# Score banks that hold two heads for half the columns, and value products that wait for half of the exponentials

## What is computed

```python
att = jnp.einsum('bhtd,bhsd->bhts', q, k) / jnp.sqrt(D)
att = att + _alibi_causal_mask(T, H, x.dtype)[None]
att = jax.nn.softmax(att, axis=-1)
y = jnp.einsum('bhts,bhsd->bhtd', att, v)
x = x + ga * (y.reshape(B, T, C) @ W_proj + b_proj)
```

## Time and profile before

| what | value |
|---|---|
| median of 3 runs | 578.42 us (578.05 to 579.37) |
| span of the profiled execution, from its first to its last instruction | 575.7 us |
| own time taken for that execution | the median, so 2.7 us lie around the span |
| first group's exponentials begin, last group's end | 52.4 and 448.7 us |
| mixture of experts on PE | from 449.4 us on |
| busy share of PE, DVE, ACT, POOL | 86%, 79%, 70%, 30% |

### The profile page before, as it was taken

How to read it: one execution, slowest core, us unless ns; L and a number is a source line. 1 busy time by engine, 2 the same in 40 slices (tenths; PEclk the granted TensorE clock), 3 DMA queues, 4 the chain that set the end, 5 groups by cost and what they waited for, 6 DMA issues and landing times.

```text
span 575.7 us, 15493 instructions
## 1 busy us (share of the span) xinstructions
PE 496.4 (86%) x5876; PEld 264.6 (46%) x5876; DVE 451.9 (79%) x775; ACT 400.9 (70%) x775; POOL 169.9 (30%) x293
## 2 busy tenths in 40 slices
PE   4756878889999999998999999989988999999970
PEld 2422323333243343333334325234433798999970
DVE  3689899989988998998998998995687555554451
ACT  4922366668888888888898887888788656555530
POOL 3310000010103102320034101047057860870864
PEclk9965599999999999999999999999899999999995
DMA  6592111000011450031310000010132222333332
GB/s 158 201 305 65 30 50 36 1 2 4 7 34 34 100 231 3 2 148 32 81 38 3 3 2 2 8 29 9 56 106 63 74 74 61 111 106 91 108 98 66
DMA packets 38263, 37.86 MB, mean 66 GB/s; under 512 B 7088, under 2 KB 33904, under 8 KB 37560
## 3 DMA queue, kind: packets, MB, share of 16 engines
q1 hardware_dynamic: 35808, 32.26, 19.5%
q0 software_dynamic: 2048, 4.20, 2.4%
q10 hardware_dynamic: 336, 0.42, 0.2%
HBM read 20.05 MB, written 16.61 MB: 64 GB/s over the span
## 4 chain that ended last, share of the span: by engine, by line
PE 59%; ACT 9%; DVE 5%; issue 3%; POOL 1%; DMA 1%; ACTq 0%; POOLq 0%; DVEq 0%
PE pv L745 18%; PE b L778 13%; PE b L852 8%; PE b L869 7%; ACT probs L1296 7%; PE b L717 6%; DVE part L1013 3%; PE b L692 3%; ACT raw L1266 1%; POOL raw L1478 1%; PE b L843 1%; PE b L647 1%; PE b L664 1%; ACT rows L1272 0%; DMA raw<-y_scratch,spots 0%
## 5 line engine op out<-in xcount | busy, mean ns | idle before, releaser
L1296 ACT ACTIVATE probs<-b 128x512 f32<-128x512 f32 (+1 forms) x576 | 298.6, 570 | 79.6 <-PE b L692 36.5
L1013 DVE TENSOR_REDUCE part<-b 128x2 f32<-128x1024 f32 (+2 forms) x320 | 327.7, 1061 | 26.8 <-PE b L717 11.8
L745 PE MATMUL pv<-probs,v_cur 128*32 128x256 f32 (+1 forms) x2432 | 176.7, 372 | 0.3 <-ACT probs L1296 0.2
L778 PE MATMUL b<-aug 55*128 55x512 bf16 (+3 forms) x640 | 114.2, 355 | 25.5 <-ACT probs L1296 21.3
L717 PE MATMUL b<-aug 52*128 52x512 bf16 (+3 forms) x640 | 117.1, 366 | 17.4 <-DVE part L1013 15.1
L778 PEld LDWEIGHTS b<-aug 55*128 55x128 bf16 x640 | 37.0, 93 | 137.6 <-ACT probs L1296 131.5
L745 PEld LDWEIGHTS pv<-probs,v_cur 128*32 128x32 f32 x2432 | 50.2, 109 | 68.3 <-issue 40.7
L852 PE MATMUL b<-hTt,inverse 128*128 128x128 f32 x424 | 56.3, 276 | 0.8 <-ACT hTt L1317 0.8
L869 PE MATMUL b<-w2T_sb,hst 128*128 x424 | 56.2, 276 | 0.8 <-ACT hst L1323 0.8
L869 PEld LDWEIGHTS b<-w2T_sb,hst 128*128 128x128 f32 x424 | 51.6, 192 | 1.2 <-issue 1.1
L852 PEld LDWEIGHTS b<-hTt,inverse 128*128 128x128 f32 x424 | 51.5, 192 | 1.0 <-issue 1.0
(11 more groups left out here) (151 smaller groups left out, 374.2 us busy)
## 6 DMA issues: line engine op xcount, KB each, us to landing
xt<-slot_scratch SPq DMA_DIRECT2D x53, 64.0 KB, 1.9
y_scratch<-aug SPq DMA_DIRECT2D x53, 64.0 KB, 1.5
slot_scratch<-slots SPq DMA_DIRECT2D x3, 1024.0 KB, 7.1
aug<-q_scratch SPq DMA_DIRECT2D x6, 384.0 KB
aug<-k_scratch SPq DMA_DIRECT2D x6, 384.0 KB
w2T_sb<-in_w2T SPq DMA_DIRECT2D x1, 2048.0 KB, 7.4
aug<-in_w1T SPq DMA_DIRECT2D x8, 256.0 KB, 2.6
q_scratch<-pieces SPq DMA_DIRECT2D x4, 384.0 KB, 2.6
```

The lines of the kernel that those rows point to most:

```text
L745: return mm(pv[32 * hh:32 * hh + 32, c0:c1], v_cur[:, kb, hh, :], probs[:, step_ % 2, hh, at_:at_ + c1 - c0], start=(kb == 0 and c0 == 0), ...
L778: done.append(mm(pair[half][:, at_:at_ + w], k_aug[g % 2][n, b, kb * P:kb * P + P], q_aug[g % 2][n, b, (j + 1) * CW - w:(j + 1) * CW], sta ...
L1013: ins = nc.vector.tensor_reduce(dst, b1[:, slot:slot + 2, at_:at_ + w], AX.X, ALU.max)
L1296: nc.scalar.activation(probs[:, p % 2, hh, 0:w], b2[:, (n2 - 1) % RING2, 0:w], ACT.Exp).then_inc(exp_done, 1)
```

## The change

A bank of scores held one head of a pair for all columns of the step. Now it holds both heads of one row tile (both low heads, or both high heads) for half of the columns, the same halves that `VALUE_PARTS` gives to the value products. `scores` is written as a generator for one row tile, and `alternate` interleaves the low and the high one, matmul by matmul. Each of the two banks waits for its own slot of the ring, just ahead of its own first matmul, and each counts itself ready after its own last matmul. The exponential reads a bank as two blocks and writes them to two heads of `probs`. Each half of the value products waits for the two exponentials that made its columns. The maxima are rewritten in the same manner (`maxima`), and their instructions come out in the order that they had. The core of the diff:

```diff
+                def alternate(low, high):
+                    for _ in zip_longest(low, high):
+                        pass
+                def mask_out(bank, half, at_, table, h, cols):
+                    k = slice(HALF * half, HALF * half + HALF)
+                    c0, c1 = cols
+                    return mm(bank[:, at_ + c0:at_ + c1], identh[k, h, :], table[k, h, c0:c1], start=False, stop=True, skip_group_check=True)
...
                 def value_products(p, b):
+                    pe.wait_ge(exp_done, HG * (NSTEP * g_ + q) + 2 * (b + 1))
                     if b == 0:
-                        pe.wait_ge(exp_done, HG * (NSTEP * g_ + q + 1))
...
-                def scores(p, b):
+                def scores(p, b, half):
                     j, kbs = STEPS[p]
-                    for half in range(2):
-                        wait_slot(half)
-                    pair = [b2[:, (len(freed) + half) % RING2, :] for half in range(2)]
+                    n = slice(HALF * half, HALF * half + ROWS2)
+                    wait_slot(0)
+                    bank = b2[:, len(freed) % RING2, :]
+                    n_exp[0] += 1
+                    freed.append((exp_done, n_exp[0]))
+                    parts = VALUE_PARTS[p][b]
                     at_ = 0
-                    for kb in kbs:
-                        w = width(j, kb)
...
-                    done[-1].then_inc(s2_ready, 2)
+                    for pair in range(PAIRS):
+                        for kb, _, c0, c1 in parts:
+                            w = c1 - c0
+                            ins = mm(bank[:, at_:at_ + w], k_aug[g % 2][n, pair, kb * P:kb * P + P], q_aug[g % 2][n, pair, j * CW + c0:j * CW + c1], start=True, stop=True)
+                            if c0 == (kb - TPC * j) * P:
+                                yield
+                                mask_out(bank, half, at_, maskT, 0, (0, HALF))
+                                yield
+                                ins = mask_out(bank, half, at_, maskT, 1, (0, P))
+                            if pair == PAIRS - 1 and kb == parts[-1][0]:
+                                ins.then_inc(s2_ready, 1)
+                            yield
+                            at_ += w
+                def scores_then_maxima(p, b, upto):
+                    alternate(scores(p, b, 0), scores(p, b, 1))
+                    pass1(upto)
...
-                            nc.scalar.activation(probs[:, p % 2, hh, 0:w], b2[:, (n2 - 1) % RING2, 0:w], ACT.Exp).then_inc(exp_done, 1)
+                            b, half = hh // 2, hh % 2
+                            at_ = VALUE_PARTS[p][b][0][1]
+                            w = sum(c1 - c0 for _, _, c0, c1 in VALUE_PARTS[p][b])
+                            out = probs[:, p % 2, :, at_:at_ + w].rearrange("p (b s) t -> p s b t", s=2)[:, half, :, :]
+                            nc.scalar.activation(out, b2[:, (n2 - 1) % RING2, 0:PAIRS * w].rearrange("p (b t) -> p b t", b=PAIRS), ACT.Exp).then_inc(exp_done, 1)
```

More of the change, by code:

```diff
@@ L13 @@
 from contextlib import ExitStack
+from itertools import zip_longest
 import numpy as np
@@ new lines, in maxima @@
+                def maxima(k, half, opens, closes):
+                    j, c, rs, b = TASKS[k % NTASK]
+                    buf = (g + k // NTASK) % 2
+                    n = slice(HALF * half, HALF * half + ROWS1)
+                    bank = b1[:, 2 * (k % SLOTS) + half, :]
+                    if opens:
+                        task_ready(k)
+                    at_ = 0
+                    for r in rs:
+                        w = (r + 1) * P if c == j else CW
+                        t = j * CW + r * P
+                        ins = mm(bank[:, at_:at_ + w], q_aug[buf][n, b, t:t + P], k_aug[buf][n, b, c * CW:c * CW + w], start=True, stop=True)
+                        if c == j:
+                            yield
+                            mask_out(bank, half, at_ + r * P, maskQ, 0, (0, P))
+                            yield
+                            ins = mask_out(bank, half, at_ + r * P, maskQ, 1, (HALF, P))
+                        if closes and r == rs[-1]:
+                            ins.then_inc(s1_ready, 1)
+                        yield
+                        at_ += w
@@ L724, in turn @@
+                def pass1(upto):
+                    for k in range(at[0], upto):
+                        alternate(maxima(k, 0, True, False), maxima(k, 1, False, True))
+                    at[0] = max(at[0], upto)
                 def turn(u):
@@ L798, in step @@
                                 take(pe, rows_in[j % 2], HG * 16)
-                            scores(p, b)
-                            pass1(min(PLAN[first][p][b], NTASK) if last else PLAN[first][p][b])
+                            scores_then_maxima(p, b, min(PLAN[first][p][b], NTASK) if last else PLAN[first][p][b])
                             if p not in START:
@@ L1285, in group @@
                     if p < NSTEP:
-                        w = PASS2[p] // HG
                         if NSTEP * g + p >= 2:
```

60 lines of the change are left out of this document (16 added, 44 removed).

## The result

The kernel after takes 563.57 us in the median of 4 runs (562.07 to 564.80), the kernel before 578.23 beside it (576.13 to 579.37). The ratio is 0.9746, with a 95% interval from 0.9717 to 0.9776. The profiled execution took 562.62 us with a span of 560.8, 14.9 less than the span before. In the kernel after, the scores stand at L795 (L778 before), their maxima at L724 (L717), masks at L697 (L692), value products at L761 (L745), exponentials at L1320 (L1296), DVE's maxima at L1034 (L1013).

The account below looks back on a forecast made before the run. Attention bound by a loop through PE and ACT of 1.20 us a half-step, PE 1.14 and DVE 1.13 close behind; 5.7 + 3.7 + 0.9 + 0.3 - 1.3 - 1.0 = 8.3 us off 578.4 gives 570.1, range 564 to 577.8.

Parts of the forecast that it names:

- (a): 116 half-steps with tasks: 7.4 us of idle above PE's floor, less 1.7 for the loop's longer half; 5.7 won.
- (b): Late in the last group, without tasks: 23 half-steps win 0.16 us each, 3.7 us.
- (e): Cost of the added score matmuls and loads on PE: 265 half-steps at 0.005 us, 1.3 us.
- (f): DVE's delays at closing a block's maxima, no longer caught up quickly: 1.0 us lost, at most 5.
- (c): Behind each step in START: 15 score waits gain a shorter reaction of 0.06 us, 0.9 us.
- The first bank ready earlier: Score loop passes through the low bank alone, complete after a 256-column matmul, 0.28 us for 0.39.
- One wait for one load: Score loads behind one wait instead of two come 0.05 us after the exponential's end instead of 0.11.
- fourth rival: PE's floor itself falls, (a) is won whole and late steps reach ACT's 0.99: below 566 us; chance 0.07.
- (d): At the attention's end, half of the last value products done earlier: 0.3 us saved.
- The diagonal: First steps of a diagonal, 16: all mask products move to the first half; net effect 0.
- Rival 3: Second pair of score loads lies open, up to 0.10 us per half-step: slower, 594.0 us; chance 0.11.
- Rivals 1 and 2: DVE or exponential takes over, 573.5 to 577.2 us, 0.17; change doesn't do what it says, about 578 us, 0.09.

Follow-up runs that it names:

- after_two_waits_high: The kernel after, with a second, long fulfilled wait ahead of the high bank's first matmul; 573.68 us, ratio to before 0.9891.
- both_waits_first: The kernel after, with both slot waits ahead of the low bank's first matmul, as before; 576.72 us, ratio to before 0.9985.
- after_one_signal: The kernel after, with both banks signalled together after the high bank's last matmul; 566.72 us, ratio to before 0.9815.
- own_waits_only: The kernel before, with each one-head bank waiting for its own slot and signalling after its own last matmul; 565.23 us, ratio to before 0.9789.
- run with four matmuls: The kernel before, with every score matmul cut into two of half the columns (does not compute the layer); 579.87 us, ratio to before 1.0049.
- after_turn_later: The kernel after, with the last turn of normed tokens and its router products one step later; 566.76 us, ratio to before 0.9785.
- low_bank_whole: The kernel after, with all low-bank matmuls ahead of all high-bank ones instead of in turn; 572.37 us, ratio to before 0.9917.

## Why the prediction was right in direction and short in size

**The sign, the bound and the loop.** That the attention is set by a loop of 1.20 a half-step, little above PE's and DVE's own, held: with the loop gone the pace is 1.11 to 1.13, just PE's, with DVE's 1.13 beside it. Of the 7.2 us that the attention won beyond the forecast, 3.5 are in (a), (b), (e) and (f) taken together, 1.7 in (c) and 2.0 in a clock that the prediction did not have.

**The step that failed first: "The first bank ready earlier."** I let the loop pass through the bank of the low heads alone because that bank is complete after a matmul of 256 columns. The runs put something else there. Own waits and signals without two-head banks give the whole gain of a middle group, two-head banks without own waits 0.5 of its 3.5 us. What counts is that the first low matmul no longer stands behind the second wait, and that the high load, with one wait, follows its exponential by 0.05 instead of 0.11. The second part alone, undone in after_two_waits_high, is 1.7 of the 3.5; both undone together are 3.0 (both_waits_first), so by difference the first is near 1.3. The early signal adds 0.3 us to a group with two-head banks and 0.7 with one-head ones.

**"One wait for one load"** was right in its number and too small in its use. In the trace the high load comes at 326.066, 0.052 behind the exponential that ends at 326.014; undone by itself, it costs 1.7 us a group. I had used it only inside the new loop and, as 0.06, in (c). From the end of the exponential to the start of the matmul that waits for it are now 0.06 us (326.014 to 326.070); before they were 0.15 (244.297 to 244.443), since the load was held by the two waits and the matmul came 0.03 behind its load.

**PE's floor.** I took 1.14 from rows in which the score loads stood 0.03 ahead of their matmuls. Once the low matmul has gone ahead or no wait is left, a load stands 0.004 ahead of it (326.038 and 326.042), and the floor is 1.12 in the mean. That is the outcome of my fourth rival, which had 0.07, though the low matmul starts only 0.03 ahead of the high one (326.042 and 326.070). The rest of that rival came as well: a plain step won 0.15, more than the 0.12 that stood above the floor, so (a) was won whole there, and late steps reach ACT's pace, 1.01 a half-step with no break in ACT. The median, 563.57, lies below the 566 that it named. The longer half of the new loop, for which I had taken 1.7 us off (a), does not show at all: from 325.417 to 326.467, the low exponentials of one step's two halves stand 1.05 apart, less than PE's half-step. The next stands 1.20 behind (327.663), but there the loads come at the floor of 0.41, so the wait is for PE's matmul and not for ACT.

**(a) to (d).** (a) and (b), less (e) and (f), came to 7.1; on and off the diagonal together 10.6 were measured. Two terms of (a) were mis-sized: the 1.7 for the longer half, and a floor of 1.14 that is 1.12, which by an estimate over the 116 half-steps is 116 x 0.02 = 2.3. A late step without other work wins 0.37, so 0.185 a half-step where (b) had 0.16. But steps 23 and 26 of the last group take 1.2 us more than before, the first with the clock at 0.66 (400 to 405 us), the second in the wait for the tokens. Steps 22 to 35 together win 2.0 of the 3.7. (c) was mis-sized: 0.06 a step for 0.18 in the middle groups. The early signal is 0.35 of those 0.72 (after_one_signal); that the early low load makes up the rest is not shown. Some of it only moves the border between two steps, since the steps behind START win 0.05 to 0.08 where a plain one wins 0.15. (d) was 0.3; the mixture's first load follows the end of the last exponential by 0.41 (433.67 to 434.08), 0.2 less than before, and the run with the old wait of the value products takes just this back.

**"The diagonal ... I take 0"** was said of the masks, which move to the first half, and for a whole group that held: own_waits_only leaves them in both halves and has the same middle group, 88.10 for 88.11, with 0.3 more on the diagonal and 0.3 less elsewhere. The miss on the diagonal is that of the loop: (a) and (b) had 2.3 us there, less what (e) and (f) take, and 4.4 were measured. Before, the masks stood in the loop through ACT in both halves. Now the half with masks is set by PE's own work and the other half by nothing but a plain half-step. In a middle group own waits and signals give 0.7 of the 1.0 won there.

**(e) and (f).** (e) was right: 0.004 measured for 0.005. The Trainium skill, "TensorE: Matmul & The Clock Gate", section "The mechanism", lets a weight load overlap a running matmul only where the row group differs. The run with four matmuls bears out the row against it: loads for the second pair of the same two tiles lie under the first. Rival 3 was out. (f), 1.0, can't be read off as one sum. In a middle group steps 8, 17 and 34 take 0.15, 0.07 and 0.07 more than before, and 13, 16, 23 and 26 win nothing; in the first and the last group four of these six steps do not lose. Of these, steps 8 and 26 wait for DVE: the loads of step 8 for 0.59 (0.43 before), those of step 26 for 0.84 as before. Why the others win nothing stays open.

**What the prediction had not at all** is the clock in the first group: 2.0 us of the profiled execution. It is not a fixed part of the change, since the same program was seen with it (113.5 us for the first group) and without it (115.7, after_turn_later). Without it, the profile of the kernel after would have been near 564.6 us (562.62 + 2.0), just within the range that began at 564. So whether the time fell a little inside or outside is luck; the mis-sized terms above are not.

**Rivals 1 and 2.** The exponential costs no more. DVE, now 8% of the chain, did not take the place: in a middle group its loads wait in no more half-steps than before, although at 1.131 it now stands above PE's 1.123 and not, as I had it, below PE's floor. The change did what it says, but more by its waits than by its banks.

## What to carry to other kernels

Where two parallel pieces of work wait for two events, put each wait directly ahead of its own piece: the piece whose event is long past then leaves the chain, and a single wait was followed 0.06 us sooner than a pair. Ask of every loop between two engines what else lies on it at the places out of the ordinary (masks, block starts): here steps in START won 0.18 and six of those on the diagonal 0.16 to 0.24, where a plain step won 0.15. When a forecast counts rows, note which kind of step each row belongs to. Count a gain in a stretch with a steady clock, and compare whole times only beside it.

## What the runs showed of the hardware

- A weight load behind two waits on PE came 0.11 us after the releasing exponential, behind one wait 0.05. A matmul that waited once and counted a semaphore up by two had a separate wait instruction in the trace and the slow 0.11; where the count was by one it had not.
- The two row tiles ran their matmuls in pairs 0.02 us apart even where the program had both low ones first; a step took 2.25 us in either order. In the trace of low_bank_whole the two loads that wait, the first of each bank, go at 335.347 and 335.371, and the first two matmuls start 0.005 and 0.004 behind them. That points to a high tile's matmul that started ahead of the second low one, which stands before it in the program; the records do not name the tile.
- The same instructions in the first group took 113.5 or 115.7 us, by when the granted clock rose from 0.50 to 1.00 (before 65 us or behind it), and waits in the last group came with falls to between 0.5 and 0.9. Such differences are as large as several of the effects measured here.
